# Score matmuls in 48 rows of fp32r on the two halves of the array, and expert weights split earlier, in an attention plus expert-choice kernel

## What is computed

```
k, q, v = proj(W_key), proj(W_query), proj(W_value)     # 16 heads of 16 channels
scores  = q k^T * hd ** -0.5, causal mask, softmax over keys
x = layernorm(x + (weight @ v) @ W_proj^T * C ** -0.5)
s = softmax(x @ router_w^T)                              # 8 experts
gate, idx = top_k(s over the 512 tokens of a sequence, 129)   # for each sequence and expert
y = (gelu(x[idx] @ w1[e] + b1[e]) @ w2[e] + b2[e]) * gate
x = layernorm(x + scatter_add(y at idx))
```

## Time and profile before

| what | value |
|---|---|
| median of 3 runs | 932.88 us (932.07 to 934.78) |
| the profiled execution's own time | 932.33 us |
| its span in the profile | 930.6 us |
| PE busy | 822.0 us, 88% of the span |
| DVE busy | 604.5 us, 65% |
| ACT busy | 532.7 us, 57% |
| POOL busy | 472.9 us, 51% |
| mean granted TensorE clock | 0.956 |
| first `st` matmul, last `st` matmul | 71.5 us, 455.5 us |
| first `up` matmul of the experts, last | 482.9 us, 895.8 us |

### The profile page before, as it was taken

One profiled execution on the slowest core, in us unless ns is written; L12 is line 12 of the kernel. 1 busy time (PEld: TensorE's weight loads), 2 busy tenths in 40 slices (PEclk: granted clock), 3 DMA queues, 4 the chain that ended last, 5 costly groups with the idle time before them and its releaser, 6 DMA issues.

```text
span 930.6 us, 17149 instructions
## 1 busy us (share of the span) xinstructions
PE 822.0 (88%) x5876; PEld 616.8 (66%) x5876; DVE 604.5 (65%) x2059; ACT 532.7 (57%) x1042; POOL 472.9 (51%) x642
## 2 busy tenths in 40 slices
PE   4668999999999999988739779999999999999990
PEld 3434445454545454434339769999999999999990
DVE  4358778878788788899656863556455454646454
ACT  2226666767585767666728333656565655655555
POOL 6336666656656565332577317454443443535343
PEclk9778999999999999999979899999999999999995
...
GB/s 139 165 151 159 103 149 124 168 93 163 112 157 120 150 108 151 157 70 3 64 108 114 121 13 69 81 92 89 76 55 124 46 138 35 143 30 54 27 137 259
DMA packets 89990, 100.52 MB, mean 108 GB/s; under 512 B 8624, under 2 KB 83376, under 8 KB 89776
## 3 DMA queue, kind: packets, MB, share of 16 engines
...
## 4 chain that ended last, share of the span: by engine, by line
PE 66%; DVE 14%; ACT 5%; issue 5%; DMA 5%; POOL 2%; SPq 1%; ACTq 0%; POOLq 0%; DVEq 0%
PE y_ps L1303 19%; PE h_ps L1289 19%; PE av_ps L741 7%; DVE n_ps L569 5%; PE st_ps L709 5%; PE n_ps L724 4%; DMA part_d<-w_raw 3%; PE stage_ps L758 3%; PE stage_ps L766 3%; PE stage_ps L800 2%; PE tp_ps L1262 2%; ACT pt L485 1%; DVE nmax L569 1%; ACT res L533 1%; PE stage_ps L791 1%
## 5 line engine op out<-in xcount | busy, mean ns | idle before, releaser
L569 DVE CUSTOM_DVE_ANT_0 n_ps<-n_ps,tri 128x512 f32<-128x512 f32 (+3 forms) x512 | 238.6, 518 | 85.0 <-PE n_ps L724 83.2
L485 ACT ACTIVATE pt<-st_ps 128x512 f32<-128x512 f32 x320 | 184.3, 602 | 66.1 <-PE st_ps L709 50.8
L1303 PE MATMUL y_ps<-w_parts,h_hi 128*128 128x256 f32 (+1 forms) x1152 | 215.2, 281 | 0.6 <-DVE w_parts L1214 0.6
L1131 ACT ACTIVATE g<-h_ps,b 128x384 f32<-128x384 f32 (+1 forms) x192 | 104.3, 543 | 169.5 <-PE h_ps L1289 169.5
L1289 PE MATMUL h_ps<-tt_hi,w_parts 128*128 128x384 f32 (+1 forms) x768 | 173.1, 328 | 22.0 <-DVE tt_lo L1177 14.1
L1103 POOL DMA_INDIRECT acc<-y,tok_no x64 | 103.2, 1613 | 146.4 <-DVE y L1238 140.0
L1303 PEld LDWEIGHTS y_ps<-w_parts,h_hi 128*128 128x128 f32 (+1 forms) x1152 | 172.8, 178 | 4.2 <-ACT h_hi L1136 0.9
L425 POOL TENSOR_SCALAR_AFFINE_SELECT pt<-pt 128x256 f32<-128x256 f32 (+1 forms) x320 | 110.7, 363 | 116.6 <-ACT pt L485 115.9
L1224 DVE TENSOR_TENSOR h_lo<-g,h_hi 128x384 fp32r<-128x384 f32 (+1 forms) x176 | 90.2, 513 | 121.2 <-ACT h_hi L1136 121.0
L1303 PE MATMUL y_ps<-w_parts,h_lo 128*128 128x256 f32 (+1 forms) x576 | 161.6, 281 | 0.0
L1289 PEld LDWEIGHTS h_ps<-tt_hi,w_parts 128*128 128x128 f32 x768 | 127.9, 191 | 22.9 <-ACT tt_hi L1122 14.3
...
...
## 6 DMA issues: line engine op xcount, KB each, us to landing
...
```

What stands on the lines that cost most here:

```text
L485: nc.scalar.activation(pt[:, slot % PT_RING, n % UP, :], st_ps[at % ST_RING][:, :], ACT.Exp, scale=S_SCALE).then_inc(exp_done, 1)
L569: ins = nc.vector.tensor_tensor_reduce(out=src[:, h, :], in0=src[:, h, :], in1=mask, scale=-1.0, scalar=-BIG_NEG, op0=ALU.add, op1=ALU.min ...
L1131: nc.scalar.activation(g[:, at % G_RING, 0:cols], h_ps[at % H_RING][:, 0:cols], ACT.Gelu, bias=b1[:, e, n:n + 1]).then_inc(g_done, 1)
L1303: ins = nc.tensor.matmul(y_ps[at % Y_RING][0:rows, 0:C], x[:, q % 2, m, toks], w[e % 2][:, m, :], start=i == 0, stop=i == len(terms) - 1)
```

## The change

Four things change together.

1. The score operands are two fp32r parts in place of three bf16 parts: three combinations of 16 channels, 48 rows, plus 2 rows for the maxima, 50. A head's stack lies in partitions 0 to 49 or in 64 to 113, by its pair (`place_of`). The matmuls then use 64 rows of the array, the upper or the lower half. The `nat` unit at a place is always of the pair whose stack is in the other half than the `st` unit's (`slot ^ 1`). `nat` has 40 units a sequence in place of 44, one at each place; the matmuls and their columns are the same (64 of `st` and 64 of `nat` a sequence), and so are DVE's 64 reductions. The columns of the weights are reordered on the host (`HEAD_ORDER`) so that the heads of one half come out together.
2. A tile of q or k needs one subtraction in place of three and two DMAs of 256 KB to `part_d` in place of three of 128 KB. The 12 reads of a stack stay 12 of 128 KB, now in rows of 2 KB, not 1 KB. The memset of the ones rows (L447) becomes a small DMA at the start.
3. Expert 0's weights are cut in eight pieces at places 12, 15, ... 33 of the last sequence (ACT, then POOL). Expert 1's weights are loaded right after it; their high parts are made in block `B` at places 1 and 12, the rest of w1 by DVE at place 11, the rest of w2 in the first expert steps.
4. In the experts' steps the first tokens are transposed and split before the last sequence's router and rows (`lastlog`, `lastrows`); the late rounds are spread 3, 8, 6 in place of 2, 7, 8, and `picked` and `joined` come two steps earlier.

The diff, cut to its core:

```diff
-K_PARTS = (0, 0, 1, 1, 0, 2)
-Q_PARTS = (0, 1, 0, 1, 2, 0)
-
-BLOCKS = len(K_PARTS) + len(Q_PARTS)
+K_PARTS = (0, 1, 0)
+Q_PARTS = (0, 0, 1)
+
+GROUP = P // 2
+BLOCKS = 2 * (len(K_PARTS) + len(Q_PARTS))
 KQ = len(K_PARTS) * D
-KM = KQ + 3
+KM = KQ + 2
...
+def place_of(h):
+
+    return h // 2 % 2, h // 4 * 2 + h % 2
+
+
+def rows_for(h, rows):
+
+    first = place_of(h)[0] * GROUP
+    return slice(first, first + rows), place_of(h)[1]
...
-N_UNITS = [(qb, h - heads + 1, heads) for h in range(H) for qb, heads in ((3, 1), (2, 1), (1, 2), (0, 4)) if (h + 1) % heads == 0]
+N_PAIR = (((0, 3, 0),), ((1, 3, 0),), ((0, 2, 0), (0, 0, 384)), ((1, 2, 0), (1, 0, 384)), ((0, 1, 0), (1, 1, 256)))
+N_UNITS = [[(2 * (slot ^ 1) + h, qb, c) for h, qb, c in unit] for slot in range(PAIRS) for unit in N_PAIR]
...
-CUTS_AT = ((B, 4), (B, 12))
+PIECES = 4
+CUT_AT = [(B - 1, 12 + 3 * piece) for piece in range(2 * PIECES)]
+NEXT_CUT_AT, NEXT_LOW_AT = ((B, 1), (B, 12)), (B, 11)
...
-                if (i, place) in CUTS_AT:
-                    yield "cut", 0, CUTS_AT.index((i, place))
+                if (i, place) in CUT_AT:
+                    yield "cut", 0, CUT_AT.index((i, place))
+                if (i, place) == (B - 1, 39):
+                    yield "load", 1, 0
+                if (i, place) in NEXT_CUT_AT:
+                    yield "cut", 1, NEXT_CUT_AT.index((i, place))
+                if (i, place) == NEXT_LOW_AT:
+                    yield "low", 1, 0
...
-                for which, stack, blocks in ((0, qst, Q_PARTS), (1, kst, K_PARTS)):
+                for which, stack, blocks in ((0, qst_b, Q_PARTS), (1, kst_b, K_PARTS)):
                     for at, part in enumerate(blocks):
-                        src = part_d[which, b % 2, part, n, :, :].rearrange("(h d) n -> d h n", d=D)
-                        sp.dma_start(stack[at * D:(at + 1) * D, b % 2, HH * n:HH * (n + 1), :], src).then_inc(stack_in[n][b % 2], 16)
+                        for first in (0, GROUP):
+                            src = part_d[which, b % 2, part, n, first:first + GROUP, :].rearrange("(h d) n -> d h n", d=D)
+                            sp.dma_start(stack[first + at * D:first + (at + 1) * D, b % 2, HH // 2 * n:HH // 2 * (n + 1), :],
+                                         src).then_inc(stack_in[n][b % 2], 16)
...
+            elif stage == "load":
+                sp.wait_ge(ahead["w1_cut"], PIECES)
+                sp.dma_start(ahead["w1_raw"][:, :, :], w1_d[1].rearrange("(k p) n -> p k n", p=P)).then_inc(ahead["w1_in"], 16)
+                sp.wait_ge(ahead["w2_cut"], PIECES)
+                sp.dma_start(ahead["w2_raw"][:, :, :], w2_d[1].rearrange("(k p) n -> p k n", p=P)).then_inc(ahead["w2_in"], 16)
+            elif stage == "x1" and n == TT - 1 and b < B - 1:
+                store_rows(b)
...
-                pool.wait_ge(parts_out[tile % 2], 48 * (tile // 2))
-                link(nc.gpsimd.tensor_tensor(qk_r[:, :], qk_f[:, tile % 2, :], parts[:, tile % 2, 0, :], ALU.subtract))
-                link(nc.gpsimd.tensor_tensor(parts[:, tile % 2, 1, :], qk_f[:, tile % 2, :], parts[:, tile % 2, 0, :], ALU.subtract))
-                nc.gpsimd.tensor_tensor(parts[:, tile % 2, 2, :], qk_r[:, :], parts[:, tile % 2, 1, :], ALU.subtract).then_inc(qk_rest, 1)
+                pool.wait_ge(parts_out[tile % 2], 32 * (tile // 2))
+                nc.gpsimd.tensor_tensor(parts_r[:, tile % 2, 1, :], qk_f[:, tile % 2, :], parts[:, tile % 2, 0, :], ALU.subtract).then_inc(qk_rest, 1)
...
-            elif stage == "cut":
-
-                pool.wait_ge(ahead[("w1_top", "w2_top")[n]], 1)
-                hi, lo = weight_parts(ahead, ("w1", "w2")[n], 0)
-                name, raw, cut = ("w1", "w2")[n], ahead[("w1_raw", "w2_raw")[n]], ahead[("w1_cut", "w2_cut")[n]]
-                for piece in range(PIECES):
-                    nc.gpsimd.tensor_tensor(piece_of(lo, name, piece), piece_of(raw, name, piece),
-                                            piece_of(hi, name, piece).bitcast(F32), ALU.subtract).then_inc(cut, 1)
+            elif stage == "cut" and b == 0:
+                w, piece = n // PIECES, n % PIECES
+                name, raw, cut = ("w1", "w2")[w], ahead[("w1_raw", "w2_raw")[w]], ahead[("w1_cut", "w2_cut")[w]]
+                hi, lo = weight_parts(ahead, name, 0)
+                pool.wait_ge(ahead[("w1_top", "w2_top")[w]], piece + 1)
+                nc.gpsimd.tensor_tensor(piece_of(lo, name, piece), piece_of(raw, name, piece),
+                                        piece_of(hi, name, piece).bitcast(F32), ALU.subtract).then_inc(cut, 1)
...
+            elif stage == "cut" and b == 0:
+                w, piece = n // PIECES, n % PIECES
+                name, raw = ("w1", "w2")[w], ahead[("w1_raw", "w2_raw")[w]]
+                act.wait_ge(ahead[("w1_in", "w2_in")[w]], 16)
+                act.wait_ge(st_done, (B - 1) * PAIRS * UP)
+                hi, _ = weight_parts(ahead, name, 0)
+                nc.scalar.activation(piece_of(hi, name, piece), piece_of(raw, name, piece), ACT.Copy).then_inc(ahead[("w1_top", "w2_top")[w]], 1)
             elif stage == "cut":
-
-                act.wait_ge(ahead[("w1_in", "w2_in")[n]], 16)
-                act.wait_ge(st_done, (B - 1) * PAIRS * UP)
-                hi, _ = weight_parts(ahead, ("w1", "w2")[n], 0)
-                nc.scalar.activation(hi, ahead[("w1_raw", "w2_raw")[n]][:, :, :], ACT.Copy).then_inc(ahead[("w1_top", "w2_top")[n]], 1)
+                act.wait_ge(ahead[("w1_in", "w2_in")[n]], 32)
+                act.wait_ge(st_done, B * PAIRS * UP)
+                hi, _ = weight_parts(ahead, ("w1", "w2")[n], 1)
+                nc.scalar.activation(hi, ahead[("w1_raw", "w2_raw")[n]][:, :, :], ACT.Copy).then_inc(ahead[("w1_top", "w2_top")[n]], PIECES)
...
+                for group in range(2):
+                    act.dma_start(qst_b[group * GROUP + KQ:group * GROUP + KM, b % 2, HH // 2 * n:HH // 2 * (n + 1), :],
+                                  nmt[HH * group:HH * (group + 1), :].bitcast(BF16)).then_inc(rows_in, 16)
...
+            elif stage == "x1" and b < B - 1:
+                finish_row(b, n)
+            elif stage == "lexp" and b < B - 1:
+                exponentials(b)
...
-                mine = nmax[:, b % 2, :, HH * n:HH * (n + 1)]
-                link(nc.vector.tensor_copy(nm3[:, :, 0, :], mine))
-                link(nc.vector.tensor_tensor(nmax_r[:, :, :], mine, nm3[:, :, 0, :], ALU.subtract))
-                link(nc.vector.tensor_copy(nm3[:, :, 1, :], nmax_r[:, :, :]))
-                nc.vector.tensor_tensor(nm3[:, :, 2, :], nmax_r[:, :, :], nm3[:, :, 1, :], ALU.subtract).then_inc(nm_parts, 1)
+                mine = nmax[:, b % 2, :, HH * n:HH * (n + 1)].rearrange("p t (g h) -> p t g h", g=2)
+                link(nc.vector.tensor_copy(nm2[:, :, :, 0, :].bitcast(F32R), mine))
+                nc.vector.tensor_tensor(nm2[:, :, :, 1, :].bitcast(F32R), mine, nm2[:, :, :, 0, :], ALU.subtract).then_inc(nm_parts, 1)
...
                 for hh, kb, c in ST_UNITS[u]:
-                    h = 2 * pair + hh
-                    ins = nc.tensor.matmul(st_ps[at % ST_RING][:, c:c + T - kb * P], kst[0:KM, b % 2, h, kb * P:(kb + 1) * P],
-                                           qst[0:KM, b % 2, h, kb * P:T], start=True, stop=True)
+                    rows, slot = rows_for(2 * pair + hh, KM)
+                    ins = nc.tensor.matmul(st_ps[at % ST_RING][:, c:c + T - kb * P], kst[rows, b % 2, slot, kb * P:(kb + 1) * P],
+                                           qst[rows, b % 2, slot, kb * P:T], start=True, stop=True)
                 ins.then_inc(st_done, 1)
...
+                for h, qb, c in N_UNITS[n]:
+                    w = (qb + 1) * P
+                    rows, slot = rows_for(h, KQ)
+                    ins = nc.tensor.matmul(n_ps[at % N_RING][:, c:c + w], qst[rows, b % 2, slot, qb * P:(qb + 1) * P],
+                                           kst[rows, b % 2, slot, 0:w], start=True, stop=True)
...
-SECOND_AT = ((0, 3), (0, 4))
-PIECES = 4
 LO_BY_POOL = 2
-PICKED_AT, JOINED_AT = (2, 3), (2, 4)
-ROWS_AT = (-1, 3)
-ROUNDS_IN = (2, 7, 8)
+PICKED_AT, JOINED_AT = (2, 1), (2, 2)
+ROWS_AT, LAST_ROWS_AT = (-1, 3), (-1, 3)
+ROUNDS_IN = (3, 8, 6)
...
+    if e == 1:
+        return -1, 4 + piece
     q, m = cut_at("cut1" if stage == "low1" else "cut2", e)
-    m += (2 if stage == "low1" else 3 if e > 1 else 5) + piece
+    m += (2 if stage == "low1" else 3) + piece
...
-    if e == 1:
-        return SECOND_AT[stage == "cut2"]
...
-        load_w1(1)
-        load_w2(1)
+        load_w1(2)
         for stage, q, n in expert_steps():
-            if stage == "low1" and n == PIECES - 1 and q + 1 < E:
+            if stage == "lastrows":
+                seen["store_rows"](B - 1)
+            elif stage == "low1" and n == PIECES - 1 and q + 1 < E:
                 load_w1(q + 1)
...
+            elif stage == "lastlog":
+                seen["exponentials"](B - 1)
```

(29 more changed lines are left out.)

159 lines of the change are left out of this document (79 added, 80 removed).

## The result

The changed kernel takes 955.0 us (median of 4 runs, 948.8 to 959.1) against 932.5 for the kernel before: 1.023 times its time, interval 1.016 to 1.030. It is slower; 886 was forecast, between 864 and 912. The profiled execution took 951.6 us (span 949.9), 19.3 more than before's 932.3.

The account below looks back on a forecast made before the run. The prediction took PE to set the pace in steady sequences and DVE in sequence 7. Its terms, -8 - 2 - 10 - 3 + 1 - 24 = -46, took the profiled 932.3 us to 886 us, range 864 to 912.

Parts of the forecast that it names:

- The score matmuls: Attention sequences: -2 us for each of sequences 1 to 5, -10 together, and -3 for sequences 0 and 6.
- width alone: Score matmuls in fp32r without overlap: 80 banks +0.8 us a sequence, matmuls of 128 columns +0 to +1.9.
- Changes of tile: Steady sequences: 29 switches between half rows and whole ones at 0.09 us each, +2.6 us a sequence.
- Overlap: Steady sequences: st and nat overlap in the two halves; PE pays +5 us without overlap, -2.2 with pairs overlapping.
- The start: Start of the program: -8 us, between -3 and -13, and -2 for the 9.84 us wait in sequence 0.
- two waits shrink by about 3.5 us each: Start: the chain's waits for writes to part_d shrink as reads use 2 KB packets, 7 us together.
- What is late next: Start: DVE is late next, with 48 of sequence 0's 64 maxima ahead of the first st.
- The turn: From attention to the experts: earlier token split and ready expert weights save 24 us, bounds -14 and -28.
- Sequence 7: Last attention sequence: +1 us for masks and exponentials that come later; DVE, the bound there, gets nothing.
- rival 4: Score matmuls: halves don't overlap at all, loads hidden; +35 us in place of -13, 934 us, chance 0.04.
- rival 5: Score matmuls: halves run in turn and every load stands in front of its matmul; 975 us, chance 0.08.
- figure for packing by rows: Score matmuls: four tiles packed on the array measured 3.07 times as fast; by it the sum would be some 17 us lower.

Follow-up runs that it names:

- e4: The changed kernel with all score matmuls over 128 rows, leaving out the separation of two heads that share rows: 938.2 us.
- e3: The changed kernel with nat in the same half of the array as st, so the two cannot overlap: 1064.8 us.
- e2: The kernel before with only the new fp32r scores in 48 rows of one half, turn to the experts as before: 968.0 us, 1.038 times before.
- e1: The kernel before with only the changes at the turn to the experts, bf16 scores as before: 910.7 us, 0.976 times before.

## Why the prediction was wrong

**The score matmuls** (forecast -2 for each of sequences 1 to 5, measured +4.1) are the step that failed, and with them the total: a term of the sum was mis-sized, and the clock was put at nothing without a reason. At full clock, from 50.3: fp32r over the whole tile +2.1 (e4), within the +0.8 to +2.7 that width alone gave. Changes of tile +3.6 (e3 at full clock, 56.0, less e4), where 29 x 0.09 = 2.6 was put. Overlap -4.8: the change has 55.8 us at 0.88 and 52.3 at 0.97, or 13.4 and 3.1 us at half clock, so 0.34 each and 51.2 at full clock, against e3's 56.0. Forecast was -7.2 (from +5 to -2.2). Together +0.9 in place of -2. This is an estimate: with e3's 0.43 the full clock's time would be 50.0 to 51.0, and the sum -0.3 to +0.7. Two things were missed. The trace of before already shows the load that isn't hidden behind a switch, in `v` behind `av`:

```profile
301.37 0.51 PE L766 MATMUL stage_ps<-w_hi,xt_hi 128*128 128x264 f32 x2
301.72 0.40 PE L766 MATMUL stage_ps<-w_hi,xt_lo 128*128 128x264 f32 x2
301.96 0.41 PE L766 MATMUL stage_ps<-w_lo,xt_hi 128*128 128x264 f32 x2
```

The pairs start 0.35 and then 0.24 us apart; only the drain ahead of `av` was priced. (29 changes at 0.2 would be 5.8 and 3.6 was measured, so not each of them pays both in full; which do was not looked at.) And PE now idles 3.8 us in place of 2.1, mostly for exponentials, which at best run no faster than before.

**The clock** was in no rival. It is the larger part: at 0.34 to 0.43 us for each of 9.2 us at half clock (the mean of sequences 1 to 5), +3.1 to +4.0 a sequence. They took 54.4 us on average in place of 50.3, +4.1 in all, so with the sums above 3.3 to 4.4 is the clock's. The prediction read PEclk only where it was below 1.00 before, and let its 1.00 in the steady stretch stand without a word. It was that of a busy PE with 96 and 99 rows active. The change halved the rows and kept PE's busy share, and nothing in the trace of before could show what that does, so it should have stood there as an unknown with bounds: 50 us a sequence at half clock would be +20.

**The start** (-8, and -2 in sequence 0) gave +0.1 and +5.5. The step "two waits shrink by about 3.5 us each" failed. Up to 72 us ACT waited for the writes to `part_d` as long as before, and the queue shows larger packets that took longer (waits before and now; the queue now, 15 to 75 us):

```profile
ACT w_raw L510 <- DMA part_d<-w_raw: 23.6, 4, 12.2
...
ACT w_raw L572 <- DMA part_d<-w_raw: 23.7, 4, 11.6
...
q1 hardware_dynamic: 5826, 10.13, 86.0%
```

A packet took 86.0% x 16 x 60 us / 5826 = 142 ns, where at most 119 was put for one of 2 KB, and the writes of a tile grew from 3 x 128 to 2 x 256 KB, which the sum leaves out. With POOL's and DVE's shorter chains ACT's last copy of a tile of q or k ahead of the first `st` comes 2.6 us earlier (52.87 against 55.46), and PE at half clock took that back: the waits left the chain because PE was later than they. "What is late next" was thus named wrongly: not DVE with the maxima, but PE at 1.2 GHz from 26.7 us on. That the rows held it there is not shown: e2, with the same scores, had 0.77 from 40 to 50 us, and its first `st` at 71.3 all the same. In sequence 0 the wait of 9.84 us is gone from the chain, but 16.2 us at half clock stand against 2.7 before, 4.6 to 5.8 us by the prices above.

**The turn** (-24) was right: -22.8 in the trace, and 22.4 us by e1, whose sequence 7 pays 3.3 of its gain. The first `up` came 19.0 us after the last `st` (27.4 - 12 = 15.4 forecast, 16.0 in e1): at a clock of 0.91 PE is busy for 12.4 us in this stretch, 10.5 in e1, which is 1.9 of the 3.0 us between them; the rest was not placed. The 6.4 and 4.6 us waits are gone: the two stretches of 35.7 and 46.6 us are now 30.6 and 37.3, at clock 1.00, -14.4 for -13 forecast. **Sequence 7** (+1) was +3.3 in e1 and +9.6 in the change, all of it with a lower clock.

**The rivals.** The number landed between rival 4 (934) and rival 5 (975), and neither mechanism is right: the halves overlap. Rival 5's step "every load stands in front of its matmul" holds for the load behind a switch only.

The Trainium skill's figure for packing by rows (page "TensorE: Matmul & The Clock Gate", section "Measured speedup vs the span model") would have made the total 17 us lower. The pairs' starts, 0.01 us apart, agree with its picture of one packed group; the kernel's time does not follow, since the groups here are two to four matmuls long, with a switch at most of their ends.
